# Cell scatters of the first expert layer moved into the weighted sum pass, one behind each lot of four gathers

## The reference

```
# weighted sum (second graph layer)
msgs = x[edge_src] * edge_val[:, None]
agg = jax.ops.segment_sum(msgs, edge_dst, num_segments=x.shape[0])
return agg @ weight
# first expert layer that sorts its rows: 6 experts, 2 for each node
h1 = relu(features @ expert_w1[e] + expert_b1[e])
h2 = relu(h1 @ expert_w2[e] + expert_b2[e])
expert_out = h2 @ expert_w3[e] + expert_b3[e]
combined = sum of the two chosen experts' outputs by routing weight
# third graph layer: three convolutions with the same normalized adjacency
msg = h[row] * norm[:, None]
out = jax.ops.segment_sum(msg, col, num_segments=n_nodes)
```

## Time and profile before

| | us |
|---|---|
| median of 3 runs | 4410.27 (4394.83 to 4424.66) |
| the profiled execution | 4444.4, of which the span of its instructions is 4442.7 |

### The profile page before, as it was taken

The page is one execution under the profiler, slowest core; times in us unless marked ns, Lnnn a source line. Parts: engine busy times, 40 slices in busy tenths (PEclk is TensorE's granted clock), DMA queues, the critical chain, the costliest instruction groups (busy, mean ns, idle before and its releaser), DMA issues. The chain is left out here.

```text
span 4442.7 us, 63030 instructions
## 1 busy us (share of the span) xinstructions
PE 3385.5 (76%) x18888; PEld 2726.1 (61%) x18888; DVE 2036.4 (46%) x5783; ACT 1545.0 (35%) x4091; POOL 2323.4 (52%) x2298
## 2 busy tenths in 40 slices
PE   3777777725857777764675399998868999998796
PEld 3555555513545555543564399997437888887696
DVE  4566555652334444433222211115346777777523
ACT  3445545411222222211221122221125666665431
POOL 3445545345546565553665443441428888785153
PEclk7878878857878888887787699999789999998698
DMA  6765555300027666651454487775449999997466
GB/s 190 212 168 144 157 142 153 89 1 25 15 63 230 220 227 220 220 166 41 134 164 153 128 247 233 250 234 161 139 146 260 265 270 266 257 268 175 146 212 208
DMA packets 491983, 777.53 MB, mean 175 GB/s; under 512 B 154330, under 2 KB 296995, under 8 KB 491395
## 3 DMA queue, kind: packets, MB, share of 16 engines
q1 hardware_dynamic: 359986, 498.14, 35.5%
q0 software_dynamic: 122608, 266.94, 24.3%
q10 hardware_dynamic: 9056, 8.43, 0.6%
HBM read 599.88 MB, written 173.38 MB: 174 GB/s over the span
## 5 line engine op out<-in xcount | busy, mean ns | idle before, releaser
L876 POOL DMA_INDIRECT ag_rows<-t_att,src_i x416 | 400.1, 962 | 390.2 <-DVE ag_msg L987 271.5
L1747 POOL DMA_INDIRECT eg_early<-t_edge,src_i x312 | 488.2, 1565 | 162.5 <-issue 91.0
L287 POOL DMA_INDIRECT t_cells<-times_seen,cell x416 | 406.1, 976 | 305.9 <-issue 125.0
L876 POOL DMA_INDIRECT sum_rows<-t_row,src_i x416 | 393.7, 946 | 293.1 <-PE ps L1197 132.3
L1067 PE MATMUL ps<-featT,ag_msg 128*128 128x128 f32 x1664 | 369.6, 356 | 110.2 <-issue 109.9
L1795 PE MATMUL ps<-eg_w,eg_rT 128*128 128x256 f32 x1664 | 435.3, 384 | 0.2 <-ACT eg_rT L1813 0.2
L1067 PEld LDWEIGHTS ps<-featT,ag_msg 128*128 128x128 f32 x1664 | 278.4, 238 | 213.9 <-issue 185.2
L1474 PE MATMUL ps<-cv_cells,cv_high 128*128 128x384 f32 (+2 forms) x1200 | 323.0, 350 | 89.6 <-DMA cv_cells<-t_cells 89.6
L973 DVE TENSOR_TENSOR att_sums<-att_sums,ps 128x384 f32 x416 | 228.6, 549 | 331.4 <-remote 179.8
L1115 PE MATMUL ps<-sum_w1g,sum_eaT 64*128 64x256 f32 x1248 | 222.9, 486 | 205.9 <-ACT sum_kept L1159 119.1
L1178 DVE TENSOR_TENSOR featT<-featT,ps 128x256 f32 x416 | 175.1, 421 | 383.0 <-remote 196.7
(11 more groups left out here) (446 smaller groups left out, 6752.9 us busy)
## 6 DMA issues: line engine op xcount, KB each, us to landing
cv_cells<-t_cells SPq DMA_DIRECT2D x225, 384.0 KB
t_pre<-sum_kept SPq DMA_DIRECT2D x156, 512.0 KB
eg_early<-t_pre SPq DMA_DIRECT2D x156, 512.0 KB
t_cells<-zeros SPq DMA_DIRECT2D x21, 1664.0 KB
cv_cells<-t_cells SPq DMA_DIRECT2D x75, 448.0 KB
xn<-in_L_ffn_W SPq DMA_DIRECT2D x57, 512.0 KB
xn<-in_L_ffn_expert_w SPq DMA_DIRECT2D x110, 256.0 KB
ag_trow<-t_dst SPq DMA_DIRECT2D x104, 256.0 KB
```

The source lines that it names most:

```text
L287: nc.gpsimd.indirect_dma_start(out=t_cells, out_offset=bass.IndirectOffsetOnAxis(ap=cell[:, c:c + 1], axis=0), in_=times_seen[:, c:c + 1], ...
L876: nc.gpsimd.indirect_dma_start(out=rows[:, j, :], out_offset=None, in_=table, in_offset=bass.IndirectOffsetOnAxis(ap=src_i[:, n:n + 1], ax ...
L1747: nc.gpsimd.indirect_dma_start(out=early[:, q % ES, n % 2, :], out_offset=None, in_=t_edge, in_offset=bass.IndirectOffsetOnAxis(ap=src_i[: ...
```

## The change

Two edits. In `edge_pass` a function is given to `gathers` that sends one cell scatter behind every fourth gather, so 104 in the pass. In the first layer of sorted experts `every=1` is left out, so `expert_tiles` sends none. Since the total is fixed at 416, the places behind the pass get less: before it 224 are sent as before, the pass sends 104, `finish_sums` 54, the choice 5, `dispatch` the last 29 instead of 30, and `collect_and_norm` finds none left instead of 48.

```diff
@@ -1133,7 +1133,10 @@
             with nc.Block() as block:
                 @block.gpsimd
                 def _(pool):
-                    gathers(pool, table, rows, GR, g.agg_ready)
+                    def cell_behind_lot(n):
+                        if n % ER == ER - 1:
+                            count_edges(pool, 1)
+                    gathers(pool, table, rows, GR, g.agg_ready, cell_behind_lot)
 
                 @block.sync
                 def _(sp):
@@ -2821,7 +2824,7 @@
             column = lambda b: lambda e, k: b[:, bass.ds(e, 1), k]
             expert_tiles(E, TS, take_row, put_row, expert, leads, len(loads),
                          [(D, io["L1_ffn_expert_w1"], column(b[0]), ACT.Relu, "ScalarE"), (D, io["L1_ffn_expert_w2"], column(b[1]), ACT.Relu, "VectorE")],
-                         (lambda e, k: w3[:, bass.ds(e, 1), k, :].rearrange("p a f -> p (a f)"), lambda e: one_row(b3, e)), every=1)
+                         (lambda e, k: w3[:, bass.ds(e, 1), k, :].rearrange("p a f -> p (a f)"), lambda e: one_row(b3, e)))
             collect_and_norm(pw)
```

## The result

| | kernel before | changed kernel |
|---|---|---|
| median of the runs | 4408.1 us (4394.8 to 4424.7, 6 runs) | 4443.6 us (4432.1 to 4447.8, 6 runs) |
| profiled span | 4442.7 us | 4446.1 us |

The ratio is 1.0068 with a 95% interval of 1.0038 to 1.0098: the change costs some 30 us (17 to 43; the medians differ by 35), which is within the 1% (44 us) that the prediction counts as no change. The forecast was 4441. The table follows the time from the first gather of the sum pass to the convolutions' first instruction. Ahead of it and behind it the code is the same, and the two profiles differ by -11.4 and +10.5 us there. A series ends here with its last gather; the changed kernel's last scatter ends 1.3 us later. All lines of after behind the edit have moved by 3.

What follows compares the result with a forecast made beforehand. The prediction took the count of POOL's indirect DMAs to bound sum pass and expert tiles. Terms 131 - 71 - 1 - 28 = +31 gave 4474 us profiled, 4441 as median from 4410.3; 8-in-10 range 4370 to 4495.

Steps and rivals of the forecast that it cites:

- What bounds the kernel: Sum pass and expert tiles: bound by the number of POOL's indirect DMAs, at 1.4 to 1.6 us apiece.
- the rule weighed in the prediction: Engines block only through semaphores, so scatters cost only POOL's issue time; would give the first rival, about 4310, chance 0.13.
- the picture of a backlog at 1.41 or 1.43 us: Each indirect DMA occupies something other engines' signals need for longer than POOL's 1.26 us issue, so signals come late.
- Sum pass, +131: 104 added scatters make 520 DMAs; pass grows from 654 to 785 us, bounds +89 to +164.
- the step from 744 us to 785: Sum pass: from 520 x 1.43 without slack to restarts at 1.49 (775) plus some 10 us of late PE.
- The rival of 1.573 for each: Sum pass pays in full, every DMA at today's 1.573 us: +164 instead of +131, 4474 us; chance 0.22.
- that of a pass at 654: Scatters hide in POOL's waits, sum pass stays at 654 us: -100, about 4310 us; chance 0.13.
- The fear that longer runs would make PE's signals late out of proportion: Sum pass: stated way to be wrong, POOL runs of ten DMAs, not eight, delaying PE's signals disproportionately; no size given.
- Expert tiles, -71: 55 scatters removed: 54 tiles fall from 4.52 to 3.2 us each, between -55 and -89.
- The cycle of three tiles: Expert tiles: if it persists, six DMAs at 1.43 plus about 1.4 us give 10.0 us, 3.33 per tile.
- The rival in which the weights hold the tiles at 4.0 us: Expert tiles gain 28 instead of 71 us, held by weights or PE's handing over: 4484 us; chance 0.12.
- Collecting block, -28: 48 scatters removed: undisturbed, ACT ends at 2470.2 instead of 2498.10; lower gain -24.

Runs made afterwards that it cites:

- the run with short fills: Changed kernel, POOL clearing 150 columns behind each of finish_sums' 54 scatters; ratio 1.0022 to the kernel before.
- The run with half the rows: Changed kernel, finish_sums' 54 scatters sending 64 numbers each and leaving out the other 64; one time, 4437.6 us.
- the spaced kernels: Kernel before and changed kernel, POOL clearing 370 columns behind each scatter of two_experts, finish_sums and collecting block; 4365.0 us (0.9907) and 4381.2 us (0.9914).
- the layout with 111 scatters: The 416 scatters redistributed: two_experts 111, finish_sums 32, pass 104, tiles 30, collecting block 24; 4353.5 us (0.9877) with fills, 4420.0 us (1.0028) without.

## Why the prediction was right, and where it was not

*What bounds the kernel.* Right: in the pass, the tiles and finish_sums time goes by the count of POOL's indirect DMAs. 1.46 us in the pass with five in a lot, 1.47 with six, and 1.64 once POOL itself takes longer. In finish_sums, where no engine waits for a scatter, they cost the adds 102.9 against 50.2 us. That speaks against the rule weighed in the prediction (the Trainium skill, Trainium Architecture — The Big Picture, "What this means for kernel authors"), by which engines block each other through semaphores alone: the measurement decides.

*How late a signal comes.* Here the picture of a backlog at 1.41 or 1.43 us is right for the end of a stream and wrong for the single signal. In the run with short fills 54 scatters at 1.365 us can pile up 54 x (1.41 - 1.365), some 2.4 us, yet one add waited 20.0 us. In the changed kernel twelve scatters were out when the eighth product was ready at 2073.59, a backlog of some 2 us, and DVE got it at 2082.73. So a signal is held up for longer than the DMAs ahead of it take; what decides that, no run shows.

*Sum pass, +131.* Mis-sized, within its bounds, by two errors that nearly cancel. The first is the step from 744 us to 785: I kept restarts of 1.49 and 10 us of late PE, but the series took 757.2, 1.456 for each, and 756.1 to 764.2 in six other executions with these 520 DMAs and no fills in the pass. A stretch of ten at 1.43 with one restart of some 0.25 us would give 14.55; that split is an estimate. The second is the base: the unchanged pass took 638.0 and 637.6 us in two other runs and 654.3 in the profile I started from. The price is 103 between the two profiles and 119 to 126 against these two runs: 28 us less for the one error, 16 more for the other. The rival of 1.573 for each is out; so is that of a pass at 654. The fear that longer runs would make PE's signals late out of proportion did not come true.

*Expert tiles, -71.* -67 from first to last rows_out, 3.28 us for a tile against 3.2, and the weights came at 229 GB/s. The cycle of three tiles persists, at 10.1 to 10.8 us where 10.0 was worked out; the mean is lower because the last eight tiles have no gather. The rival in which the weights hold the tiles at 4.0 us is out.

*Collecting block, -28.* First add to the convolutions 69.5 to 41.4: -28.1, by the chain as it was read. dispatch moved by nothing that can be read.

*The sum.* +31 was forecast, +35 measured between the medians and 30 by the ratio. With +119 to +126 for the pass the parts give +23 to +30 (-67, -1 and -28), inside the measurement's 17 to 43; with the +103 of the two profiles they would give +7, outside it. So the mechanism gives the sum, but the nearness of 4441 to 4443.6 is partly luck, by the two errors in the pass. The profile of before was a long execution, 35 us above the median of its runs (that of after 3): its attention pass, unchanged code, took 783.0 us, as the four runs on the slower chip did (781.5 to 784.5), where after and all others took 767.5 to 774.0. That and the 654.3 make its span 27 us longer, and its part behind the convolutions' start was 10.5 us shorter. The run with half the rows, else the changed kernel, was 28 us above its kernel before (one execution). The pair in the spaced kernels gives +15.6 us from the first gather to the convolutions, and 16 us between medians from two chips but 3 us by the ratios; it doesn't settle the figure more closely than the interval.

*Not seen at all:* what late signals cost in two_experts, with 144 scatters in six streams: I read only the stages that the diff touches. With fills alone the stage is 22 us shorter; in the layout with 111 scatters it takes 185.1 us with fills and 231.3 without.

## What to carry to other kernels

Count POOL's indirect DMAs per stage and multiply by their real period (here 1.41 to 1.47 us), not by the duration that the profile shows for one (0.96): where that fills a stage, moving them only moves their cost, and it is cheapest where other engines have their own work for as long. A stream sent faster than that made the other engines' signals late here, while POOL itself seemed idle or early. Something small between two of them gave 0.9% where POOL had time to spare, and cost 8 to 97 us in the pass, where it had none. Before summing stage lengths from one profile, hold its span against the median of the runs, and an unchanged stage against the same stage in another run.

## What the hardware showed that I had not expected

- A slower POOL made the kernel faster: 0.42 us of clearing behind each of 246 scatters, some 70 us more of POOL's time, and 44 us less in all. In finish_sums, at periods of 1.26 and 1.365 us, DVE stood idle for up to 20 us with its product ready; at 1.55 and 1.65 us it did so for none of 25.
- The price does not depend on the rows: 64 instead of 128 changed the issue from 0.96 to 0.90 us, and the end of the late signals not at all (1.402 us for each scatter, 1.405 with 128).
- The lateness of the first signals is small and grows in steps (2.8, 5.2, 6.6, 8.7, 11.6, 15.0 us in finish_sums after the change), and it is over 7.9 us after POOL's last issue (11.1 with half the rows, 4.8 with 32 scatters).
- What the shared thing is, no run here shows, but the traces narrow it. It is not the moving of data: in finish_sums the last packet of POOL's DMAs ended at 2128.27, 0.8 us behind the last issue, and DVE's last late add came at 2135.35. And the trace itself loses semaphore updates of these DMAs (16 for each) while signals are late: with 32 scatters it holds 114 of 512 without fills and 323 with them. That points at the updates, and leaves it open whether the recording, which every run here had, takes part.
